# A four-block transformer kernel: attention features from three split parts stacked on 96 rows by on-chip copies, norm chain moved up in the step

## The chip, the core and the metric

The kernel runs on one core of a Trainium2 chip. The metric is the device time of one execution in microseconds (us), lower is better. The core has a matrix engine (TensorE, PE in the profile, whose weight loads are listed apart as PEld), a vector engine (VectorE, DVE), a scalar engine (ScalarE, ACT), a general engine (GpSimd, POOL) and a queue engine (SyncE, SP) that here only issues DMAs. Each engine works through its own list of instructions in order; they meet through semaphores, on which an instruction waits until a count is reached.

## What is computed

Four blocks, each followed by a residual add and a layer norm: a state-space mixer, a dense feed-forward, a linear attention with random features, and a feed-forward with 8 routed and 2 shared experts. The change is in the attention. Its reference, cut to what matters (batch 4, 1024 tokens, width 256, 16 heads of 16; M = 32 directions, R = 2 nodes, so 64 features for each head):

```python
def _features(x, omega, quad_nodes, quad_weights):
    xn = x / jnp.maximum(jnp.linalg.norm(x, axis=-1, keepdims=True), 1e-12)
    proj = jnp.einsum('bhtd,rhdm->rbhtm', xn, omega)
    s = quad_nodes[:, None, None, None, None]
    arg = jnp.clip(proj * jnp.sqrt(2.0 * jnp.maximum(s, 0.0)) - s, -20.0, 20.0)
    feat = jnp.exp(arg) / np.sqrt(M).astype(np.float32)
    feat = feat * jnp.sqrt(jnp.maximum(quad_weights, 0.0))[:, None, None, None, None]
    return jnp.transpose(feat, (1, 2, 3, 0, 4)).reshape(B, H, T, R * M)
qkv = x @ Wqkv + bqkv
q, k, v = jnp.split(qkv, 3, axis=-1)
qf = _features(q, omega, quad_nodes, quad_weights)
kf = _features(k, omega, quad_nodes, quad_weights)
# causal linear attention over chunks of 128 tokens:
#   ctx = qf . cumsum(kf v), den = max(qf . cumsum(kf), 1e-6), out = ctx / den
return out @ Wout + bout
```

## The kernel before

The program runs in phases with a barrier of all engines between them: `phase_mixer` (the first two blocks), `phase_attention`, `phase_shared` and `phase_experts`. A matrix product in fp32 accuracy is made of fp32r parts: an operand x is split into a high part (a copy by ACT) and a low part (x minus high, by DVE), and three products high.high, high.low and low.high are added up in PSUM (`PARTS`).

`phase_attention` goes through 8 steps of 128 tokens x 4 batch entries (`body(i)`, with a ninth body that empties the pipeline). A step has 8 turns t = 0 to 7, one for each pair of heads. In turn t the matrix engine computes

- `features` of pair t: queries and keys of two heads against the directions, 2 banks of 512 columns;
- `scores` and `turn_keys` of pair t-1, then `context` of pair t-2;
- and the step's other work, the "x steps", placed by the table `SLOTS_OF_X` at three points of a turn: A after the features, B after the scores, C after the context.

The x steps are: `FT` 0, 1 (turn the input rows), `FQ` 0 to 3 (project queries and keys, one for each batch entry), `FV` (values), `FN` 0 to 3 (turn the normed queries and keys into columns: 0 and 2 hold pairs 0 to 3 of queries and keys, 1 and 3 pairs 4 to 7), `BO` (turn the context back), `BC` and `BW` (output projection). `FT`, `FQ`, `FN` 0 and `FN` 2 are made one step ahead. Two PSUM banks, used in rotation, hold the results; DVE's `x_evac` frees them (`x_free`), for `FT`, `FN` and `BC` after ACT's `x_high`.

Between `FQ` and `FN` lies the norm chain. POOL squares queries and keys in two halves (L1308, after `FQ` 1 and `FQ` 3), DVE sums them (`squares`, L1670), makes a first guess of the inverse root (`norm_guess`, L1675 to L1677) and three Newton steps (`norm_newton`, L1680 to L1682), POOL multiplies (L1313, two instructions, one for `FN` 0 and 2 and one for `FN` 1 and 3). DVE's list in a turn is: `clip` of pair t (L1651, reads the features' banks), x step A, `mask` of pair t-1 (L1656), x step B, `new_state`, x step C, with the norm pieces between. ACT's list is: `x_high` of A, `exponentials` of pair t (L1520), `key_rows`, `x_high` of B, `context_out`, `x_high` of C.

There is one pair of feature banks, one pair of score banks and one context bank: `features` of the next pair waits for this pair's `clip`, `scores` for the last `mask`. The normed columns lie in one tile `qkt` of 128 rows (8 heads x 16) by parts, with keys rolled by 32 rows so that the two products of a pair use different rows. `features` (L1419) then issues six matmuls on 32 rows each:

```python
rows = [slice(2 * HD * at, 2 * HD * (at + 1)) for at in (t % 4, (t + 1) % 4)]
for c, (lp, rp) in enumerate(PARTS):
    for q in range(2):
        mm = pe.matmul(ps[:, FB + q, :], om[rows[q], lp, t, :], qkt[rows[q], rp, KD * q + t // 4, :],
                       start=c == 0, stop=c == 2)
```

Beside this POOL and ACT split the routed experts' weights, four blocks of 512 KB in each of steps 1 to 6 (POOL: L1287, then a store L1289 and a load L1291 by DMA). SP loads the next rows, stores finished rows, and at the phase's start loads the six blocks of shared weights (L1246), which the next phase uses.

## Time and profile before

| | us |
|---|---|
| median of 3 runs | 1459.89 (1459.82 to 1463.75) |
| the profiled execution | 1448.13, span 1446.5 |
| `phase_mixer` | 0 to 325.6 |
| `phase_attention` | 325.6 to 773.6 |
| `phase_shared` and `phase_experts` | 773.6 to 1446.5 |
| one step of attention (544.04 to 599.70) | 55.66 |
| PE busy in that step | 53.60 |
| DVE, ACT, POOL busy in that step | 43.36, 27.61, 26.60 |

The profile shows one execution, 11.8 us under the median of the runs without one. Its rows give for each engine when a group of like instructions started, how long it was busy, and in brackets how long the engine had been idle before and what released it. A matmul's end is modelled, so for groups on PE the distance from start to start says what a group costs. Busy time of an engine says little by itself; what counts is whether something waits for it.

### The profile page before, as it was taken

How to read it: one execution, taken by the hardware profiler on the slowest of the kernel's cores; microseconds unless marked ns; L12 is line 12 of the kernel's file. 1: busy time of each engine (PE TensorE's matmuls, PEld its weight loads, DVE VectorE, ACT ScalarE, POOL GpSimd, SP SyncE). 2: the span in 40 equal slices, each digit the busy share in tenths (PEclk: the TensorE clock that was granted, in tenths of full speed). 3: DMA queues.
4: the chain of work that ended last, by engine and by line, in shares of the span. 5: the costliest groups of instructions: out<-in, count | busy, mean ns of one | idle time of the engine just before them, and what ended most of it. 6: DMA issues, size and time to landing. Idle time of an engine off the chain costs nothing. (4 is left out here: it accounts for less than half of the span.)

```text
span 1446.5 us, 33923 instructions
## 1 busy us (share of the span) xinstructions
PE 1371.3 (95%) x12256; PEld 1190.8 (82%) x12256; DVE 914.3 (63%) x1944; ACT 684.4 (47%) x1257; POOL 551.6 (38%) x503
## 2 busy tenths in 40 slices
PE   6989999989999999999998999999999999999994
PEld 5778888877677777777777988888899999999984
DVE  4666767676776877877774464444555555555547
ACT  2356667544545455445444433223355555555533
POOL 0144555442254354454310006422344444444421
PEclk9799999998999999999999999999999999999997
DMA  6333333105133133233115204633788888888885
GB/s 223 128 136 123 111 133 128 52 15 181 45 100 120 57 117 123 65 131 102 45 60 219 104 30 162 263 111 122 188 227 233 234 233 234 233 234 234 248 258 213
DMA packets 103869, 216.12 MB, mean 149 GB/s; under 512 B 18544, under 2 KB 74224, under 8 KB 96624
## 3 DMA queue, kind: packets, MB, share of 16 engines
q1 hardware_dynamic: 79552, 159.87, 33.8%
q0 software_dynamic: 23088, 54.31, 13.1%
q8 instruction: 47, 0.77, 0.2%
q10 hardware_dynamic: 1152, 0.93, 0.2%
q14 instruction: 30, 0.25, 0.1%
HBM read 150.23 MB, written 64.84 MB: 149 GB/s over the span
## 5 line engine op out<-in xcount | busy, mean ns | idle before, releaser
L2637 PE MATMUL ps<-e_xhl,s_whl 128*128 128x256 f32 x1848 | 245.7, 282 | 0.0
L2637 PEld LDWEIGHTS ps<-e_xhl,s_whl 128*128 128x128 f32 x1848 | 231.0, 189 | 0.2 <-issue 0.2
L2019 PE MATMUL ps<-s_xhl,s_whl 128*128 128x512 f32 x660 | 164.5, 398 | 1.4 <-PEq L1108 1.4
L2468 POOL DMA_INDIRECT xs<-e_y,e_slot_id x78 | 122.1, 1566 | 90.5 <-ACT e_y L2502 71.4
L492 POOL TENSOR_TENSOR b_hhl<-b_h,b_hhl 128x512 fp32r<-128x512 f32 x64 | 94.7, 1482 | 139.7 <-ACT b_hhl L756 118.3
L2019 PEld LDWEIGHTS ps<-s_xhl,s_whl 128*128 128x128 f32 x660 | 122.1, 190 | 26.5 <-issue 1.8
L2616 PE MATMUL ps<-s_whl,e_ghl 128*128 128x256 f32 x936 | 139.3, 285 | 0.6 <-issue 0.6
L2716 DVE TENSOR_TENSOR e_g<-ps,e_act_h 128x256 f32<-128x256 f32 x156 | 66.2, 424 | 112.8 <-ACT e_act_h L2515 112.8
L2616 PEld LDWEIGHTS ps<-s_whl,e_ghl 128*128 128x128 f32 x936 | 121.8, 189 | 0.8 <-issue 0.7
L589 PE MATMUL ps<-b_w,b_hhl 128*128 128x256 f32 x768 | 105.3, 287 | 6.3 <-DVE b_turned_rows L862 5.6
L2515 ACT ACTIVATE e_act_h<-ps 128x256 f32<-128x256 f32 x156 | 60.1, 385 | 107.9 <-PE ps L2637 102.4
L589 PEld LDWEIGHTS ps<-b_w,b_hhl 128*128 128x128 f32 x768 | 99.2, 192 | 11.7 <-issue 6.0
L576 PE MATMUL ps<-b_xhl,b_w 128*128 128x512 f32 x384 | 104.4, 407 | 0.1
L1520 ACT ACTIVATE c_qf<-c_cf,fc 128x512 f32<-128x512 f32 x64 | 46.2, 722 | 117.9 <-DVE c_cf L1651 117.9
L1287 POOL TENSOR_TENSOR c_elo<-c_eraw,c_ehi 128x1024 fp32r<-128x1024 f32 x24 | 57.2, 2385 | 107.0 <-ACT c_ehi L1537 99.3
L2730 DVE TENSOR_TENSOR e_ghl<-e_g,e_ghl 128x256 fp32r<-128x256 f32 x156 | 67.8, 435 | 41.8 <-ACT e_ghl L2525 41.8
L2009 PE MATMUL ps<-s_whl,d_ghl 128*128 128x256 f32 x672 | 90.2, 283 | 1.8 <-DVE d_ghl L2251 1.6
L2009 PEld LDWEIGHTS ps<-s_whl,d_ghl 128*128 128x128 f32 x672 | 86.7, 188 | 6.2 <-ACT d_ghl L2105 1.8
L2245 DVE TENSOR_TENSOR d_g<-ps,d_act_h 128x512 f32<-128x512 f32 x56 | 38.7, 690 | 83.5 <-PE ps L2019 69.8
L1651 DVE TENSOR_SCALAR c_cf<-ps,fc 128x1024 f32<-128x1024 f32 x64 | 85.6, 1338 | 4.8 <-PE ps L1419 4.4
L2525 ACT ACTIVATE e_ghl<-e_g 128x256 fp32r<-128x256 f32 x156 | 64.7, 415 | 46.8 <-DVE e_g L2716 46.8
L2461 POOL CAST s_whl<-wall 128x1024 fp32r x38 | 39.5, 1041 | 119.3 <-PE ps L2616 109.4
(384 smaller groups left out, 2737.2 us busy)
## 6 DMA issues: line engine op xcount, KB each, us to landing
s_whl<-wlo SPq DMA_DIRECT2D x38, 1024.0 KB, 5.0
s_whl<-wlo SPq DMA_DIRECT2D x38, 512.0 KB, 3.7
c_eraw<-in_expert_w POOLq DMA_DIRECT2D x24, 512.0 KB, 4.9
wlo<-c_elo POOLq DMA_DIRECT2D x24, 512.0 KB, 3.0
wall<-in_expert_w SPq DMA_DIRECT2D x8, 1536.0 KB, 9.2
xg<-b_zeros POOLq DMA_DIRECT2D x13, 780.0 KB, 3.9
e_xr<-xg SPq DMA_DIRECT2D x39, 260.0 KB, 3.8
x<-rows_out SPq DMA_DIRECT2D x16, 512.0 KB, 3.2
```

Source lines behind the costliest of these rows:

```text
L492: gp.tensor_tensor(hhl[:, m % 4, 1], h[:, m % 4], hhl[:, m % 4, 0].bitcast(F32), ALU.subtract).then_inc(s["hlo_ready"], 1)
L576: mm = pe.matmul(ps[:, H + m % 2, :], w1s[:, wp, kd, m * P:(m + 1) * P], xhl[:, k, xp, kd, :], start=q == 0, stop=q == 3 * KD - 1)
L589: mm = pe.matmul(ps[:, O + b // 2, lo:lo + D], hhl[:, m % 4, hp, b * P:(b + 1) * P], w2s[:, wp, m, :], start=m == 0 and q == 0 and b % 2 = ...
L1651: ve.tensor_scalar(cf[:, u % 2], ps[:, FB:FB + 2, :], fc[:, HIGH], fc[:, LOW], ALU.min, ALU.max).then_inc(s["clip_done"], 1)
L2009: mm = pe.matmul(ps[:, O + b // 2, (b % 2) * D:(b % 2 + 1) * D], ghl[:, m % 4, gp_, b * P:(b + 1) * P], whl[:, wp_, m // HM, lo:lo + D], s ...
L2019: mm = pe.matmul(ps[:, H + 2 * (m % 2) + w, :], whl[:, wp, e, lo:lo + P], xhl[:, k, xp, kd, :], start=q == 0, stop=q == 3 * KD - 1)
L2468: gp.indirect_dma_start(xs, bass.IndirectOffsetOnAxis(ap=slot_id[:, i, b:b + 1], axis=0), y[:, k, b, :], None, compute_op=ALU.add).then_in ...
L2525: act.activation(ghl[:, m, 0], g[:, m], ACT.Copy).then_inc(s["ghi_ready"], 1)
L2616: mm = pe.matmul(ps[:, O + k, b * D:(b + 1) * D], ghl[:, m, gp_, b * P:(b + 1) * P], whl[:, k, wp_, lo:lo + D], start=m == 0 and q == 0 an ...
L2637: mm = pe.matmul(ps[:, H + m, w * SLOT:(w + 1) * SLOT], whl[:, k, wp, lo:lo + P], xhl[:, k, xp, kd, :], start=q == 0, stop=q == 3 * KD - 1)
L2716: ve.tensor_tensor(g[:, m], ps[:, H + m, SLOT:2 * SLOT], act_h[:, m], ALU.mult).then_inc(s["g_ready"], 1)
L2730: ve.tensor_tensor(ghl[:, m, 1], g[:, m], ghl[:, m, 0].bitcast(F32), ALU.subtract).then_inc(s["glo_ready"], 1)
```

## The change

- `features` multiplies once for each bank: a stationary operand of 96 rows (high, low, high of the directions, prepared by the host as one block repeated four times on 128 rows and split so that rows 32 to 63 hold the low part) against a moving operand `fs` of 96 rows that holds high, high, low of a pair's normed columns. Two matmuls for a pair in place of six.
- `fs` is filled by DMAs. `FN` results are split into a tile `stage`; `stack_pair` then copies, for each pair, three blocks of 32 rows x 2 x 512 values (128 KB each) from `stage` to `fs` on SP's queue: 12 copies for each half of a step (`stack(i+1, 0)` after `FN` 2, `stack(i, 1)` after `FN` 3). `features` waits for its pair's three copies, and ACT's `x_high` of `FN` 1 and of `FN` 0 waits until the four pairs copied last from `stage` have landed.
- The x steps are placed anew: `FQ` 0 to 3 in turns 2 and 3 (before in 3 and 4), `FN` 0 and 2 in turn 6 (before in 7), `BO` 0 and 1 one turn later. `squares` and `norm_guess` stand in turn 4, the Newton steps in turn 5. On POOL the squares come before the third weight block.
- The tiles `gm`, `bs`, `st`, `bt`, `ct` of the mixer, and `stage`, share memory with rows that are used later. The first four pairs of step 0 are copied at the mixer's end. Four of the six blocks of shared weights are loaded at the end of attention, since `fs` uses their place. SP's stores of finished rows come one body later.

Cut to its core:

```diff
+def stack_pair(sp, ahead, t):
+    g = t % QUAD
+    for n, part in enumerate((0, 0, 1)):
+        sp.dma_start(ahead.fs[t // QUAD][n * MF:(n + 1) * MF, g].bitcast(F32), ahead.stage[g * MF:(g + 1) * MF, part].bitcast(F32)).then_inc(ahead.stacked[t], 16)
...
+                if is_(i, STEPS + 1):
+                    sp.wait_ge(s["fn_lo"], 2)
+                    for t in range(QUAD):
+                        stack_pair(sp, ahead, t)
...
-                      2: ((A_, "FT", 0), (B_, "FT", 1), (C_, "BO", 3)),
-                      3: ((A_, "FQ", 0), (B_, "FQ", 1), (C_, "BC", 1)),
-                      4: ((A_, "FQ", 2), (B_, "FQ", 3), (C_, "BW", 0)),
-                      5: ((A_, "BW", 1), (C_, "BO", 0)),
-                      6: ((A_, "BO", 1),),
-                      7: ((A_, "FN", 0), (B_, "FN", 2))}
+                      2: ((A_, "FT", 0), (A_, "FT", 1), (B_, "BO", 3), (C_, "FQ", 0)),
+                      3: ((A_, "FQ", 1), (B_, "FQ", 2), (C_, "FQ", 3), (C_, "BC", 1)),
+                      4: ((B_, "BW", 0),),
+                      5: ((A_, "BW", 1),),
+                      6: ((A_, "BO", 0), (B_, "FN", 0), (C_, "FN", 2)),
+                      7: ((C_, "BO", 1),)}
...
+            def stack(i, half):
+                k1 = (i, "FN", 3) if half else (i - 1, "FN", 2)
+                sp.wait_ge(s["x_free"], x_index(*k1) + 1)
+                for t in range(QUAD * half, QUAD * (half + 1)):
+                    if not isinstance(i, int) or i > 0:
+                        sp.wait_ge(s["feat_done"], 2 * (PAIRS * (i - 1) + t + 1))
+                    stack_pair(sp, ahead, t)
...
+                if last_rows(i):
+                    sp.wait_ge(s["feat_done"], 2 * PAIRS_ALL)
+                    for n in range(2, NCH):
+                        load_shared(n)
...
+                pe.wait_ge(stacked[t], STACKED * (i + 1))
                 wait(pe, "clip_done", n)
...
+                for q in range(2):
+                    pe.matmul(ps[:, FB + q, :], om[0:STACK, t, :], fs[t // QUAD][0:STACK, t % QUAD, q, :],
+                              start=True, stop=True).then_inc(s["feat_done"], 1)
...
+                        if name == "FN" and a < KD:
+                            for before in range(QUAD * (1 - a), QUAD * (2 - a)):
+                                act.wait_ge(stacked[before], STACKED * (i + 1))
...
+                    if front and t == 4:
+                        squares(norm, i + 1, 0)
                     if front and t == 5:
-                        squares(norm, i + 1, 1)
-                        norm_guess(norm)
                         norm_newton(norm, False)
...
                     if front and t == 4:
-                        squares(norm, i + 1, 0)
+                        squares(norm, i + 1, 1)
+                        norm_guess(norm)
```

Where instructions stand now, at the three places that matter. On PE in the loop's body of attention, turn 6 of a step (features, then `c_ot` is `BO`, `c_qf` scores, `ident,c_kf` turned keys, `c_va` to `c_sm` the context). Before:

```order
L1419 MATMUL ps<-s_qkt,early 128x512 x6
L1235 REGISTER_ALU
L1395 MATMUL ps<-ident,c_ot 128x128 x4
L1425 REGISTER_ALU
L1431 MATMUL ps<-c_qf,c_kf 128x128 x8
L1437 MATMUL ps<-ident,c_kf 128x128 x4
L1451 MATMUL ps<-c_va,c_kr 64x32 x8
```

The same turn in the changed kernel (`s_fs` is the stacked operand, `s_sq` the normed rows that `FN` turns):

```order
L1459 MATMUL ps<-s_fs_53,early 128x512 x2
L1254 REGISTER_ALU
L1439 MATMUL ps<-ident,c_ot 128x128 x4
L1463 REGISTER_ALU
L1469 MATMUL ps<-c_qf,c_kf 128x128 x8
L1475 MATMUL ps<-ident,c_kf 128x128 x4
L1254 REGISTER_ALU
L1429 REGISTER_ALU
L1433 MATMUL ps<-ident,s_sq 128x128 x4
L1489 MATMUL ps<-c_va,c_kr 64x32 x8
```

`FN` 0 now stands in turn 6 between the turned keys and the context; before, it stood in turn 7 behind the features. On DVE, from the clip of turn 4 to the clip of turn 5, in the changed kernel (`s_nrm<-s_sq` is `squares`, `c_sm` the mask, `s_zz` the evacuation of `BW` 0):

```order
L1697 TENSOR_SCALAR c_cf<-ps,fc 128x1024
L1714 REGISTER_ALU
L1716 TENSOR_REDUCE s_nrm<-s_sq 128x64
L1702 TENSOR_TENSOR c_sm<-ps,s_tri 128x1024
L1647 REGISTER_ALU
L1675 TENSOR_TENSOR s_zz<-ps,c_xb 128x512
L1708 TENSOR_TENSOR c_state<-ps,c_state 128x128
L1714 REGISTER_ALU
L1716 TENSOR_REDUCE s_nrm<-s_sq 128x64
L75 ISA
L1721 TENSOR_SCALAR s_nrm<-s_nrm 128x128
```

Both sums now come in turn 4, one of them ahead of the mask; before, the second came behind the clip of turn 5. On SP the end of the mixer and the start of attention, before:

```order
L452 DMA x<-rows_out 128x4x256
L244 UNCONDITIONAL_BRANCH
L1237 UNCONDITIONAL_BRANCH
L1240 DMA s_tri<-in_masks 128x128
L1241 DMA c_bout<-in_bout 128x256
```

and in the changed kernel:

```order
L466 DMA x<-rows_out 128x4x256
L229 DMA s_fs_52<-s_stage 32x1024 x12
L258 UNCONDITIONAL_BRANCH
L1256 UNCONDITIONAL_BRANCH
L1259 DMA s_tri<-in_masks 128x128
L1260 DMA c_bout<-in_bout 128x256
```

Twelve copies stand ahead of the barrier that ends the mixer.

## Rows read from the trace of the kernel before

**Rows 1.** Windows: us of window, busy of each engine, PEclk (granted clock), DMA share, GB/s.
```profile
544.04:599.70 55.66, 53.60 (x713) 40.45 (x714) 43.36 (x82) 27.61 (x48) 26.60 (x31) 1.00 0.31 104
```
**Rows 2.** Timeline (start, us, engine line op): PE, turn 3, features, FQ 0, scores.
```profile
563.73 0.97 PE L1419 MATMUL ps<-s_qkt,early 32*128 32x512 f32 x6
564.82 1.66 PE L1358 MATMUL ps<-early,s_xts 128*128 128x512 f32 x6
566.41 1.16 PE L1431 MATMUL ps<-c_qf,c_kf 64*128 64x128 f32 x16
```
**Rows 3.** Timeline: PE, BC 0 of turn 1, features of turns 5 and 6.
```profile
550.86 0.66 PE L1398 MATMUL ps<-ident,c_cr 128*128 128x128 f32 x4
...
580.76 0.96 PE L1419 MATMUL ps<-s_qkt,early 32*128 32x512 f32 x6
...
587.28 0.96 PE L1419 MATMUL ps<-s_qkt,early 32*128 32x512 f32 x6
```
**Rows 4.** Timeline: PE, turn 7 and the start of the next step.
```profile
592.84 0.96 PE L1419 MATMUL ps<-s_qkt,early 32*128 32x512 f32 x6 [0.54 <-DVE c_cf L1651]
593.73 0.66 PE L1389 MATMUL ps<-ident,s_sq 128*128 128x128 f32 x4
594.89 1.16 PE L1431 MATMUL ps<-c_qf,c_kf 64*128 64x128 f32 x16 [0.50 <-DVE c_sm L1656]
...
599.70 0.49 PE L1419 MATMUL ps<-s_qkt,early 32*128 32x512 f32 x2 [0.88 <-DVE s_qkt L1599]
```
**Rows 5.** Timeline: DVE, turn 5: clip, second sum, Newton step, mask.
```profile
582.60 1.34 DVE L1651 TENSOR_SCALAR c_cf<-ps,fc 128x1024 f32<-128x1024 f32 x1
...
584.45 1.21 DVE L1670 TENSOR_REDUCE s_nrm<-s_sq 128x64 f32<-128x1024 f32 x1
...
586.48 0.29 DVE L1680 SCALAR_TENSOR_TENSOR s_nrm<-s_nrm 128x128 f32<-128x128 f32 x1
...
587.46 1.22 DVE L1656 TENSOR_TENSOR c_sm<-ps,s_tri 128x1024 f32<-128x1024 f32 x1
```
**Rows 6.** Timeline: POOL, normed rows, and the store of the fourth weight block.
```profile
590.78 3.83 POOL L1313 TENSOR_TENSOR s_sq<-s_qk,s_nrm 128x1024 f32<-128x1024 f32 x2 [9.07 <-DVE s_nrm L1682]
...
597.60 0.60 POOL L1289 DMA_DIRECT2D wlo<-c_elo  x1 [0.67 <-POOL c_elo L1287]
```
**Rows 7.** Timeline: ACT in turn 0, high parts of FN 1 and FN 3, exponentials.
```profile
545.64 0.60 ACT L1513 ACTIVATE s_qkt<-ps 128x512 fp32r<-128x512 f32 x1 [2.03 <-PE ps L1389]
546.78 0.72 ACT L1520 ACTIVATE c_qf<-c_cf,fc 128x512 f32<-128x512 f32 x1 [0.54 <-DVE c_cf L1651]
...
548.50 0.58 ACT L1513 ACTIVATE s_qkt<-ps 128x512 fp32r<-128x512 f32 x1
```
**Rows 8.** Timeline: DVE, low part of FN 2.
```profile
598.87 0.69 DVE L1599 TENSOR_TENSOR s_qkt<-ps,s_qkt 128x512 fp32r<-128x512 f32 x1 [0.64 <-ACT s_qkt L1513]
```
**Rows 9.** One line's DMAs of 128 KB on SP: ns min/median/max, and landing.
```profile
L388 SPq DMA_DIRECT2D b_grown<-drow x16: 472/508/633, 26.4 to 214.6; - x16
...
DMA to landing us min/median/max: 2.7/3.3/11.1
```
**Rows 10.** One line's stores of 8 and 24 KB on SP, and landing.
```profile
L393 SPq DMA_DIRECT2D arow<-b_turned_rows x2: 343/350/356, 21.2 to 71.3; - x2
...
DMA to landing us min/median/max: 1.4/1.4/1.4
```
**Rows 11.** Timeline: end of the mixer, last low parts on DVE, first features.
```profile
323.00 1.27 DVE L1030 TENSOR_TENSOR s_qkt<-ps,s_qkt 128x512 fp32r<-128x512 f32 x2
...
325.60 1.65 PE L1419 MATMUL ps<-s_qkt,early 32*128 32x512 f32 x6 [3.60 <-PEq L1103]
```
**Rows 12.** Timeline: PE, first router product of the phase behind attention.
```profile
777.75 1.92 PE L1988 MATMUL ps<-wall,d_xts 128*128 128x8 f32 x16 [0.89 <-DMA d_ones<-in_masks]
```
**Rows 13.** Windows around the mixer's end: the granted clock is the third value from the right.
```profile
316.00:320.00 4.00, 0.37 (x4) 0.17 (x2) 3.85 (x6) 0.00 (x0) 2.87 (x2) 0.91 0.00 0
320.00:326.00 6.00, 2.37 (x10) 2.00 (x12) 4.25 (x5) 1.20 (x2) 1.97 (x2) 0.50 0.00 0
```

99 lines of the change are left out of this document (51 added, 48 removed).

## The prediction

> **What bounds the kernel now.** I read the page first, then the windows, then the timeline of one steady step, engine by engine. In the step from 544.04 to 599.70 PE is busy 53.60 of 55.66 us at the full granted clock, DVE 43.36 [rows 1]. So attention runs at PE's pace, and a matmul taken away is worth its start-to-start distance as long as nothing else comes late. The reader should see second where PE does wait in the step: 0.54 us for the clip and 0.50 us for the mask in turn 7, 0.88 us for the low part of `FN` 2 at the next step's start [rows 4], and 0.2 us in turn 3, where the features take 1.09 us to the next start [rows 2] against the 0.89 of turn 7 [rows 4]. These 2.1 us are spots where DVE is a turn behind: from the clip at 582.60 on its rows leave no gap [rows 5] until the norm chain's end releases POOL at 590.78 [rows 6]. The change takes work off PE and none off DVE, and puts the norm chain closer to its user. The waits decide, not the count of matmuls.
>
> **The features.** Six matmuls on 32 rows cost 593.73 - 592.84 = 0.89, say 0.90 us [rows 4] (two run beside each other, since they use different rows). The two new ones use the same 96 rows, so they follow each other. The nearest row is `FQ`: six matmuls of 128x512 take 566.41 - 564.82 = 1.59 us, 0.265 each [rows 2], so two take 0.53. Saving 0.37 a pair, 64 pairs: -23.7 us. The Trainium skill, TensorE: Matmul & The Clock Gate, Part 1, gives 215.7 ns from start to start for such a matmul at the warm clock; by that figure two take 0.43 and the saving would be 30 us. The row in this kernel is slower and I stay with it. As bounds I take 0.30 to 0.45 a pair, 19 to 29 us.
>
> The unstalled step of before is 55.66 - 2.1 = 53.5 us; less 8 x 0.37 it is 50.6. If nothing else were late the seven steps after the first would give this: 23.7 + 6 x 2.1 = 36 us. Now what comes late.
>
> **The norm chain against `FN` 0.** `FN` 0 needs POOL's first product, which needs the last Newton step. Time on PE, from the start of turn 5: before, turn 5 takes 587.28 - 580.76 = 6.52 us [rows 3]; now 0.37 less, and without `BO` 0 (some 0.6), so 5.55. In turn 6 PE reaches `FN` 0 after features 0.53, `BO` 0 0.6, scores 1.1 and turned keys 0.6: 8.4 us after turn 5's start. On DVE the list from the clip of turn 4 to the chain's end is two clips with an evacuation each (582.60 to 584.45, 1.85 each), two sums and the first guess (584.45 to 586.48 is one sum with the guess, 2.03, and 1.2 for the other), two masks (1.15 each), three Newton steps (587.46 - 586.48, 0.98 each) and two state updates with a wait for ACT (0.9 in all) [rows 5]: 3.7 + 3.2 + 2.3 + 2.9 + 0.9 = 13.0. It can begin when `BC` 1's low part is done, 1.4 us into turn 4 (an ACT copy of 0.60 and a DVE subtraction of 0.69 and the hops [rows 7, 8]). Turn 4 is also some 5.55 us. So the chain ends 1.4 + 13.0 - 5.55 = 8.85 us into turn 5, POOL's first product takes half of 3.83 [rows 6], and `FN` 0 can start at 10.8 in place of 8.4: **a new wait of 2.4 us**. Before, the chain ended at 590.7 and `FN` 0 came only at 593.73 [rows 4, 6]. The squares on POOL are no limit: they now stand ahead of the third weight block. Six steady steps: +14.4. Bounds 1 to 3.5 a step.
>
> **The copies.** `FN` 2 is now PE's last work in turn 6; its low part is done 1.4 us into turn 7. Turn 7 before takes 599.70 - 592.84 = 6.86, of which 1.4 are waits [rows 4]; less 0.37, and with one `BO` in place of two `FN`, it is 4.6 us. So 3.2 us are left for the first copies, and none of this kind is in the trace. Nearest rows: 128 KB on SP take 0.51 us to issue (0.47 to 0.63) and 2.7 to 3.3 us to land out of HBM [rows 9]; small stores take 0.35 us and 1.4 us [rows 10]. I take 0.55 an issue, back to back, and 2.5 us to land (nearer to the row of the same size, a bit below it because both ends are on the core). Pair 0: 0.2 + 2 x 0.55 + 2.5 = 3.8, so the step starts 0.6 us late. All four pairs: 0.2 + 11 x 0.55 + 2.5 = 8.75, 10.15 us into turn 7. Until then ACT's list stands still at the high part of `FN` 1; behind it are queued the exponentials of pair 0, `key_rows` of pair 7 and the high part of `FN` 3. From there: ACT copy 0.65, exponentials and key rows 548.50 - 546.78 = 1.72, copy 0.58 [rows 7], low part 0.69 and hops 0.2: `FN` 3's bank is free 3.85 us later, 14.0 us into turn 7. PE wants that bank for `BC` 0, before 6.82 us into the step (550.86 - 544.04 [rows 1, 3]), now 6.1, that is 4.6 + 6.1 = 10.7 into turn 7. **PE loses 3.3 us** at each passage to a new step, 0.6 at the start and the rest at `BO` 2 and `BC` 0. Seven passages: +23. Bounds: 0 with small-store numbers, 6 with a landing later by 3 us. The 12 copies of the other half have two turns more and are hidden by turns 1 to 3; what would cost is only their place on SP's queue, ahead of the load of rows for `FT`, which is due a step later. The low part of `FN` 1 holds DVE up too (clip, then this, then the mask): the mask of pair 7 is then due in turn 1, where PE waits already.
>
> **The edges.** The last low part of the mixer ends at 324.3 and the first features start at 325.6 [rows 11]. Now SP first issues 12 copies, 12 x 0.55 = 6.6 us less the 0.4 in which the others arrive: the barrier is late by +6.2 (4 to 7.5). At the other end four loads of 512 KB follow attention's last store; the router's first product waited at 777.75 for a small load issued behind the barrier [rows 12], and that now queues behind 2 MB: +2.5 (1 to 5). Step 0 has no `BW` and `BC`, so PE reaches `FN` 0 even earlier, but it waited there before as well: +1 (0 to 3). Moving the mixer's tiles, the host's new layout and the fewer rows of the low part of the directions cost nothing on any path.
>
> **The sum**, against the profiled execution (1448.13): -23.7 - 6 x 2.1 (12.6) + 14.4 + 23 + 6.2 + 2.5 + 1 = +10.8. I take off 1.5 for turn 3's and turn 7's waits in step 0 and step 7, which partly go too: +9.3. The profiled execution lies 11.8 us under the median; I put the same difference on the median: 1459.89 + 9.3 = **1469.2 us**, 0.6% slower. Two measurements of this kernel can be told apart from about 0.3%, 4.4 us.
>
> **Rivals.** (1) *The copies are quick.* With 0.35 to issue and 1.7 to land, the step starts on time, all four pairs are there after 0.2 + 3.85 + 1.7 = 5.75 us, and PE loses 0.4 at a passage; the first edge shrinks to 12 x 0.35 - 0.4 = 3.8: -23.7 - 12.6 + 14.4 + 2.8 + 3.8 + 2.5 + 1 - 1.5 = -13.3, 1446.6, faster. For it: the copies never touch HBM. Against: 12 in a row, and the row of the same size. This is the other side, and it decides at the landing of the twelfth copy: each us earlier than mine is worth 7 us, until 5.5 us.
> (2) *The copies are slow.* POOL's fourth weight block stands behind both products. Before, its store came 597.60 - 590.78 = 6.8 us after they began [rows 6]; now they begin 8.85 us into turn 5, so its store and load, 1 MB, start some 2 us into turn 7, just when the copies do. If the twelfth lands 3 us later still, 7 x 3 = +21: 1490. The Trainium skill, SBUF — State Buffer, section on the DMA port swizzle, says that a transfer on 32 partitions reaches 8 of the 16 ports and gives 189 GB/s for 1 MiB; by that the twelve copies (1.57 MB) would need 8.3 us of transfer alone where my issues take 6.6, so it speaks for this rival and against the change. No row here shows a copy between 32 partitions.
> (3) *The norm chain is in time*, because DVE starts turn 4 earlier or POOL's product is quicker: then 6 x 2.4 fall away, 1455. Against: DVE's rows are without a gap and their durations do not vary.
> (4) *The clock falls.* It went from 1.00 to 0.50, half of full speed, after PE had been idle for most of 316 to 320 [rows 13]. My waits are 2.4 us and shorter, so mostly not; if they do it at some passages, 2 to 3 us each, 1480 to 1490.
>
> **How the numbers follow.** Forecast 0.41 (1462 to 1477), rival 1 0.23, rival 2 0.19, rival 3 0.11 (half of it over 0.3% faster), rival 4 0.06. Faster by over 0.3% (under 1455.5): 0.23 + 0.05 = 0.28. Within 0.3%: 0.06 from rival 3 and 0.09 from the low end of the forecast, 0.15. Slower: 0.57. The range reaches from inside rival 1 to rival 2's time: 1445 to 1490.
>
> **What the profile after would show.** Two matmuls of 96x512 with 0.53 us to the next start (wrong if 0.6 or more). In turn 6 a wait of PE before `FN` 0 released by POOL's product, 2.4 us. DVE without a gap from turn 4 to the end of turn 5. SP: twelve issues of 0.5 us after `FN` 2, landing 2 to 3 us each. ACT idle in turn 0 until the twelfth lands, then PE waiting before `BO` 2 and `BC` 0, 3 us in all. First features 6 us later than 325.6. A step of 50.6 + 2.4 + 3.3 = 56.3 us. If the step is 53 us, the copies or the chain were quicker than I have it; if it is 59, the copies share the engines with POOL's transfers.

## The result and the profile after

The changed kernel takes **1516.43 us** (median of 4 runs, 1514.39 to 1517.87); the kernel before took 1460.68 us (1459.82 to 1463.75, 4 runs) beside it. The ratio is 1.0377, 95% interval 1.0357 to 1.0397: 3.8% slower. The forecast was 1469.2 with a range to 1490, so the direction was right and the size was missed by 47 us.

The profiled execution of the changed kernel, and its steady step (from the first features of one step to the first of the next), stretch by stretch: length, busy time of PE, PEld, DVE, ACT and POOL, granted clock, DMA share, GB/s. The first line is the counterpart of [rows 1].

```profile
569.78:630.92 61.14, 54.52 (x680) 42.84 (x681) 43.55 (x80) 27.64 (x48) 26.48 (x30) 0.92 0.51 146
618.00:625.50 7.50, 7.40 (x74) 5.56 (x74) 4.19 (x6) 2.62 (x6) 6.80 (x6) 0.54 0.18 70
640.00:646.00 6.00, 6.00 (x86) 5.16 (x85) 3.88 (x6) 3.15 (x5) 1.68 (x1) 1.00 0.92 205
```

A step takes 61.14 us, 5.5 more than before, with 33 matmuls fewer in the record (680 for 713). PE is *busier* than before (54.52 against 53.60 us): matmuls were taken away, and where the granted clock falls to half of full speed those that are left last longer. The second stretch is such a place: mean granted clock 0.54. The third is one in which only the copies move data, at 205 GB/s.

What the clock takes shows in the six steps from the second on, in the changed kernel and then in a run that is told below, e_two_matmuls, which issues as many matmuls of the same shapes, in the old slots and without the copies:

```profile
381.94:750.20 368.26, 322.19 (x4081) 253.16 (x4081) 257.85 (x466) 163.78 (x284) 155.35 (x165) 0.92 0.50 141
```

```profile
373.96:696.73 322.77, 296.39 (x4084) 235.44 (x4080) 255.69 (x467) 163.49 (x285) 155.01 (x165) 1.00 0.31 101
```

For the same number of matmuls PE is busy 322.2 us at a mean granted clock of 0.92 and 296.4 us at 1.00: 26 us more. It stands idle 46.1 us in place of 26.4. (A matmul's end is modelled, so this is about right and not exact.)

What PE waits for, over the whole program (in total, times, longest):

```profile
PE ps L1459 <- DMA s_fs<-s_stage: 20.5, 7, 4.8
PE ps L1433 <- POOL s_sq L1357: 13.2, 6, 2.2
PE ps L1459 <- PEq L1122: 11.6, 1, 11.6
PE ps L1439 <- DVE s_xts L1645: 7.0, 5, 1.5
PE ps L1439 <- DVE s_stage L1645: 5.8, 2, 3.5
...
PE ps L2035 <- DMA d_ones<-in_masks: 4.3, 1, 4.3
```

Line by line: the features wait for the copies; `FN` 0 waits for POOL's product; the first features wait behind the barrier after the mixer; `BO` 3 waits for `FT` 0's bank and `BO` 2 for `FN` 3's; the router waits for a small load. The same in order of time, from turn 6 on, on PE (start, us, line, what is multiplied, and in brackets the wait before and its end):

```profile
615.25 0.66 PE L1475 MATMUL ps<-ident,c_kf 128*128 128x128 f32 x4
618.10 0.72 PE L1433 MATMUL ps<-ident,s_sq 128*128 128x128 f32 x4 [2.20 <-POOL s_sq L1357]
618.75 1.07 PE L1489 MATMUL ps<-c_va,c_kr 128*64 128x32 f32 x16
...
623.67 1.96 PE L1469 MATMUL ps<-c_qf,c_kf 64*128 64x128 f32 x16
625.57 0.66 PE L1475 MATMUL ps<-ident,c_kf 128*128 128x128 f32 x4
...
630.92 0.72 PE L1459 MATMUL ps<-s_fs,early 96*128 96x512 f32 x2 [2.38 <-DMA s_fs<-s_stage]
631.48 0.60 PE L1433 MATMUL ps<-ident,s_sq 128*128 128x128 f32 x4
632.01 1.94 PE L1469 MATMUL ps<-c_qf,c_kf 64*128 64x128 f32 x16
```

The reader should see two waits of 2.2 and 2.4 us, and after each the same instructions at about half speed for some microseconds: the sixteen score matmuls take 1.96 and 1.94 us, against 1.16 elsewhere in the step. Beside it POOL, SP and ACT:

```profile
622.92 0.59 POOL L1331 DMA_DIRECT2D wlo<-c_elo  x1 [0.67 <-POOL c_elo L1329]
623.53 0.53 POOL L1333 DMA_DIRECT2D c_eraw<-in_expert_w  x1
...
624.37 21.91 SPq L229 DMA_DIRECT2D s_fs<-s_stage  x24
...
635.13 0.60 ACT L1560 ACTIVATE s_stage<-ps 128x512 fp32r<-128x512 f32 x1 [6.72 <-DMA s_fs<-s_stage]
```

POOL's store and load (1 MB) are issued 1.45 and 0.84 us ahead of the first copy. That copy is issued at 624.37, the third has landed at 630.92 (6.5 us, where the forecast had 0.55 x 2 + 2.5 = 3.6), and the twelfth at 635.1 (10.8 us, forecast 8.55). ACT's list stands still for 6.72 us. All copies by line, issue time and time to landing (min, median, max), and who waited:

```profile
L229 SPq DMA_DIRECT2D s_fs<-s_stage x192: 507/591/1971, 323.5 to 768.4; - x192
...
  ACT s_stage L1560: 52.6, 7
...
DMA to landing us min/median/max: 2.2/2.4/9.4
```

The issue (0.59) and the undisturbed landing (2.4 us) are what I had assumed (0.55 and 2.5). The landing up to 9.4 is not.

One number must be settled first. The first profile of before lay 11.8 us under its median. **e_before_again** is that kernel once more.

> The kernel before once more, unedited, for a second profiled execution. The first one (1448.1 us) lay 11.8 us under the median of the others, and the profiles of the changed kernel, of the norm part alone and of the stacking alone all show some 11 us in the shared phase in which PE's instructions start about 0.7 us apart without waiting for a semaphore, which the first profile of before doesn't show. If this stretch belongs to the kernel before as well: span near 1459, the stretch in the shared phase, attention as before (55.65 us a step). If it is a cost of the change: span near 1447 again, without it.

It took 1472.58 us (one run, span 1470.9), while the kernel before beside it had a median of 1466.0. Its attention is the old one (steps of 55.64 us, last features at 751.31 against 751.63); all the difference lies behind. The same stretch in the shared phase, first execution, then this one:

```profile
880.00:900.00 20.00, 20.00 (x114) 17.42 (x113) 8.44 (x12) 5.53 (x9) 15.61 (x16) 1.00 0.52 178
```

```profile
880.00:900.00 20.00, 11.55 (x47) 7.84 (x46) 2.77 (x4) 1.86 (x3) 15.44 (x17) 0.81 0.28 99
...
PE ps L2009 <- issue: 10.5, 11, 2.2
```

PE waits for no semaphore there, its instructions just come slowly. So this stretch belongs to the kernel before as well, and my carrying the 11.8 us over to the median was right. It goes with the chip, it seems: the experiments were made in five groups, each on a chip of its own, and the kernel before had medians of 1461.7, 1466.0, 1461.9, 1446.3 and 1465.4 us in them. In the fourth group all 16 executions of before took 1441 to 1451 us, and the four traces from it (e_late_only, e_late_warm, e_late_edges, e_all_mends) lack the stretch; in the other four groups before took 1459 to 1472 us and every trace has it. What makes it is not known. Below I therefore compare **ratios to the kernel before beside the run**, and 0.1% is 1.5 us. The last column of the table is a second measure, which leaves out all that lies behind attention: the time from the first to the last features in the trace of the run. The two traces of the kernel before give 426.0 and 426.1 us there, on times that lie 24 us apart.

### The profile page after: what moved, and what is told of

Read it like the earlier page. It is cut to its first block and busy times, and to the rows that moved or that the text cites. A ratio compares the mean times of both kernels' runs of the same rounds, so it can differ in the third digit from the quotient of the medians.

```text
span 1516.3 us, 33677 instructions
## 1 busy us (share of the span) xinstructions
PE 1378.1 (91%) x12000; PEld 1205.1 (79%) x12000; DVE 914.5 (60%) x1944; ACT 683.9 (45%) x1257; POOL 547.4 (36%) x503
## 3 DMA queue, kind: packets, MB, share of 16 engines
q0 software_dynamic: 23088, 54.31, 12.6%
## 5 line engine op out<-in xcount | busy, mean ns | idle before, releaser
L2066 PE MATMUL ps<-s_xhl,s_whl 128*128 128x512 f32 x660 | 170.3, 406 | 5.3 <-PEq L1127 2.6
L2056 PEld LDWEIGHTS ps<-s_whl,d_ghl 128*128 128x128 f32 x672 | 87.9, 191 | 12.6 <-issue 7.3
L1469 PEld LDWEIGHTS ps<-c_qf,c_kf 64*128 64x128 f32 x1024 | 69.8, 207 | 24.3 <-issue 18.6
L1469 PE MATMUL ps<-c_qf,c_kf 64*128 64x128 f32 x1024 | 82.6, 306 | 6.3 <-DVE c_sm L1702 4.1
```

Of the source, the lines that this page charges most:

```text
L1469: mm = pe.matmul(ps[:, SC + h, cols], kf[f, u % 4, cols], qf[f, u % 4, cols], start=True, stop=True)
L2056: mm = pe.matmul(ps[:, O + b // 2, (b % 2) * D:(b % 2 + 1) * D], ghl[:, m % 4, gp_, b * P:(b + 1) * P], whl[:, wp_, m // HM, lo:lo + D], s ...
L2066: mm = pe.matmul(ps[:, H + 2 * (m % 2) + w, :], whl[:, wp, e, lo:lo + P], xhl[:, k, xp, kd, :], start=q == 0, stop=q == 3 * KD - 1)
```

## The experiments

| run | ratio to before | 95% interval | first to last features, us |
|---|---|---|---|
| the kernel before | 1 | | 426.0 |
| the changed kernel | 1.0377 | 1.0357 to 1.0397 | 462.4 |
| e_norm_only | 1.0130 | 1.0101 to 1.0159 | 440.2 |
| e_two_matmuls | 0.9902 | 0.9876 to 0.9928 | 409.8 |
| e_stack_only | 1.0404 | 1.0377 to 1.0430 | 467.3 |
| e_pool_early | 1.0390 | 1.0351 to 1.0429 | 462.3 |
| e_warm | 1.0376 | 1.0354 to 1.0397 | 465.4 |
| e_spread | 1.0406 | 1.0362 to 1.0450 | 464.1 |
| e_two_queues | 1.0185 | 1.0166 to 1.0204 | 443.0 |
| e_bo_first | 1.0386 | 1.0363 to 1.0409 | 467.7 |
| e_shared_early | 1.0309 | 1.0287 to 1.0332 | 462.2 |
| e_late_only | 1.0286 | 1.0262 to 1.0309 | 448.7 |
| e_late_fn | 1.0146 | 1.0123 to 1.0169 | 429.0 |
| e_best | 1.0155 | 1.0124 to 1.0185 | 439.6 |
| e_late_warm | 1.0086 | 1.0064 to 1.0109 | 420.5 |
| e_late_edges | 1.0103 | 1.0081 to 1.0126 | 439.2 |
| e_all_mends | 1.0045 | 1.0030 to 1.0060 | 428.2 |
| e_ft_apart | 1.0025 | 1.0004 to 1.0045 | 423.1 |
| e_final | 1.0031 | 1.0013 to 1.0050 | 424.4 |

**The three parts of the change apart.** First the two matmuls, without copies:

```diff
-                for c, (lp, rp) in enumerate(PARTS):
-                    for q in range(2):
-                        mm = pe.matmul(ps[:, FB + q, :], om[rows[q], lp, t, :], qkt[rows[q], rp, KD * q + t // 4, :],
+                for q in range(2):
+                    pe.matmul(ps[:, FB + q, :], om[0:96, 0, t, :], qkt[0:96, 0, KD * q + t // 4, :],
```

> The kernel before with its six feature matmuls on 32 rows replaced by two on 96 rows that read the keys and queries where they already lie: no copies, no stacking, old slots and norm chain. It leaves out the low parts of the product and takes rows of the wrong heads, so its output is not the features' product; it times PE's side of the change by itself. Forecast's term: 0.37 us a pair (0.33 by the rows of the changed kernel), 64 pairs, -21 to -24; if DVE's lateness of 2.1 us a step stays or grows (DVE is a turn behind in turns 3, 4 and 7), less. Step 52.7 to 53.5 with the waits staying, 1437 to 1443 us; if all that is saved on PE turns into waits for DVE, 1455 to 1461.

0.9902, so **-14 us**. Its steady step, and two waits of turn 6:

```profile
588.86:642.92 54.06, 49.44 (x680) 39.23 (x681) 43.05 (x82) 27.50 (x48) 26.55 (x31) 1.00 0.33 107
...
632.05 1.16 PE L1427 MATMUL ps<-c_qf,c_kf 64*128 64x128 f32 x16 [1.21 <-DVE c_sm L1652]
...
636.07 0.74 PE L1417 MATMUL ps<-s_qkt,early 96*128 96x512 f32 x2 [0.54 <-DVE c_cf L1647]
```

PE's busy time falls from 53.60 to 49.44, 4.16 us or 0.52 a pair, more than my 0.37. But the step falls by 1.6 only: PE idles 54.06 - 49.44 = 4.62 us in place of 2.06, for DVE. Over attention its waits for the mask (`c_sm`) rise to this, where the kernel before had 4.5 us, 8 times:

```profile
PE ps L1427 <- DVE c_sm L1652: 14.4, 14, 1.4
```

Second, the norm chain and the slots alone, with the squares and the guess on DVE and the weight blocks on POOL where the change has them:

```diff
-                      6: ((A_, "BO", 1),),
-                      7: ((A_, "FN", 0), (B_, "FN", 2))}
+                      6: ((A_, "BO", 0), (B_, "FN", 0), (C_, "FN", 2)),
+                      7: ((C_, "BO", 1),)}
...
-                    split_expert_weights(i, range(1, EPER - 1))
+                    split_expert_weights(i, range(1, 2))
...
+                    split_expert_weights(i, range(2, EPER - 1))
```

> The kernel before with one part of the change alone: the new slots of the projections (FN 0 and FN 2 in turn 6, both FT in point A of turn 2), the norm chain moved up on DVE and the norm products' place on POOL. Features stay six matmuls on 32 rows, no copies. Forecast's terms: FN 0 then waits for POOL's first product, about 2.0 us a step (PE comes to it 0.7 us later than in the changed kernel, since its features are longer), the 0.9 us wait for the low part of FN 2 at a step's start goes: 6 x 1.1 = +7, 1467 us, step 56.8. Rival (what the trace of the changed kernel suggests): the wait also brings the clock down to half for some 6 us of PE work (+2 a step), and BO 3 waits 1.4 us for FT 0's bank: 6 x 4.5 = +27, 1487 us, step 60. If the norm part were harmless and all of the loss lay in the copies: 1455 to 1460.

1.0130, **+19 us**, between the forecast's +7 and the rival's +27. The step is 57.8 us in place of 55.65:

```profile
609.48:667.29 57.81, 54.87 (x714) 41.29 (x714) 43.54 (x81) 27.71 (x48) 26.54 (x30) 0.97 0.30 99
...
657.99 0.66 PE L1391 MATMUL ps<-ident,s_sq 128*128 128x128 f32 x4 [1.98 <-POOL s_sq L1315]
...
660.00 1.08 PE L1464 MATMUL ps<-c_sm,c_va 128*32 128x128 f32 x16
```

The sum by rows of that step: +1.98 for `FN` 0, +0.96 for `BO` 3's bank (a wait at 627.88), +1.27 busy time at a lower clock, less before's 2.06 of waits, all of which are gone here: +2.15, and the step is 57.81 - 55.66 = 2.15 longer. The wait for POOL is what I forecast; the clock and the bank I had left out.

Third, the stacking in the old slots: the changed kernel with the old `SLOTS_OF_X`, norm chain and POOL order, the diff above read backwards.

> The changed kernel with the old slots, the old place of the norm chain on DVE and of the products on POOL: only the stacking is left. FN 2 is then at point B of turn 7, so the first copies can be issued only some 4 us later than in the changed kernel. No FN 0 wait, no BO 3 wait. If the landing of the copies is what costs (6.5 us to the third, in place of my 3.6): a wait of about 6 us at each step's start with the clock falling after it, less the 2.2 + 1.4 + 1.5 that the norm part costs in the changed kernel: step about 62 to 63, 1525 us. If the norm part costs most of the 56 us that the changed kernel lost: 1490 us or less. By my recorded forecast (landing 2.5 us, no clock fall) the wait would be 3.5 us at the start, the rest as before: step 57 to 58, 1480 us.

1.0404, **+59 us**, worse than the whole change: the third copy comes 7 us after PE wants it.

```profile
635.32 1.21 PE L1457 MATMUL ps<-s_fs,early 96*128 96x512 f32 x2 [6.96 <-DMA s_fs<-s_stage]
```

Features -14 and norm chain +19 make +5; the whole change is +55, so some 50 us come with the copies (and the two edges, which every kernel with copies has). The parts don't add up: features and stacking in the old slots are +59, with the norm part's 19 that would be 78, and the whole is 55. Moving `FN` 2 ahead costs 19 us by itself and nothing here, where it lets the copies start sooner.

**POOL's megabyte, the clock, the order of the copies.** Moving POOL's fourth block ahead of the norm products:

```diff
-                    split_expert_weights(i, range(2, EPER - 1))
+                    split_expert_weights(i, range(2, EPER))
...
-                if not isinstance(i, int) or 1 <= i < LAST:
-                    split_expert_weights(i, range(EPER - 1, EPER))
```

> The changed kernel with one edit: POOL's fourth weight block (store and load, 1 MB) comes ahead of the norm products, in the 8 us in which POOL waits for DVE's chain, not behind them, where it starts 0.2 us before the first copies. Theory A (POOL's megabyte in front delays the copies, my rival 2): the third copy lands some 4 us after its issue in place of 6.5, the wait at the step's start falls from 2.4 us to nearly 0 with its clock fall, ACT's high part of FN 1 comes 2 us sooner: 3 to 4 us a step, 6 x 3.5 = -21, about 1495 us. Theory B (the copies are slow by themselves, half rate for 32 rows and 0.59 us an issue): within 4 us of the changed kernel, 1512 to 1520. If POOL's split of the block is too long for the gap, FN 0 waits longer and the time goes up: 1525.

No gain: 1.0390. But the trace shows that the theory was right on the third copy and blind to what is late next:

```profile
623.23 14.23 SPq L229 DMA_DIRECT2D s_fs<-s_stage  x14
...
626.92 0.73 PE L1457 MATMUL ps<-s_fs,early 96*128 96x512 f32 x2 [0.70 <-DMA s_fs<-s_stage]
634.12 0.65 PE L1437 MATMUL ps<-ident,c_ot 128*128 128x128 f32 x4 [2.19 <-DVE s_stage L1643]
636.23 1.11 PE L1440 MATMUL ps<-ident,c_cr 128*128 128x128 f32 x4 [0.93 <-DVE s_stage L1643]
...
632.66 0.60 ACT L1558 ACTIVATE s_stage<-ps 128x512 fp32r<-128x512 f32 x1 [6.18 <-DMA s_fs<-s_stage]
```

With POOL's transfer out of the way the third copy lands 3.7 us after the first issue (my 3.6), and PE waits 0.70 in place of 2.38. The twelfth still lands after 9.4 us, ACT still stands for 6.18, and PE pays 2.19 + 0.93 at `BO` 2 and `BC` 0. The forecast had this second wait as the main one; POOL's block only hid it in the changed kernel. After it the clock falls, as the row of `BC` 0 shows: the four transposes of `c_cr` take 1.11 us, against 0.66 in [rows 3].

The clock: 8 matmuls of 96x512 added ahead of `FN` 0's wait and 8 ahead of the step's first wait for a copy.

```diff
+                    if name == "FN" and a == 0:
+                        for _ in range(8):
+                            pe.matmul(ps[:, xp, :], om[0:STACK, 0, :], xts[0:STACK, 0, 0, :], start=True, stop=True)
```

> The changed kernel with 8 added matmuls of 96x512 (2.1 us at full clock, results overwritten) ahead of FN 0's wait for POOL and ahead of each later step's first wait for the copies, so that PE works in about the time in which it stood. The waits themselves end when they ended before. Theory C (the clock's fall to half after these two waits costs about 3 us a step, 1.2 to 1.9 us for work that takes 0.6 to 1.1 otherwise): granted clock 0.98 or more in attention in place of 0.92 to 0.94, 6 x 2.5 = -15, 1500 us. If the clock had no part in the loss: 1516 or, where the added work outlasts the wait, up to 1522.

No gain either: 1.0376. The clock stays at 1.00 after `FN` 0, and the time is taken back at the next wait, which is 3.43 us although 2.1 us of added work stand ahead of it (in the changed kernel 2.38 with nothing ahead; the clock falls after it in both):

```profile
622.11:625.11 3.00, 3.00 (x54) 2.24 (x54) 1.54 (x3) 1.31 (x3) 2.97 (x2) 1.00 0.00 0
...
633.63 1.22 PE L1465 MATMUL ps<-s_fs,early 96*128 96x512 f32 x2 [3.43 <-DMA s_fs<-s_stage]
```

The first copy is issued 4.5 us after `FN` 0's start (620.91 to 625.37) in place of 6.3, and the third lands 8.3 us after that in place of 6.5: POOL's megabyte, issued at 625.75, comes when it came before, and the copies end when it lets them.

Two mends each without effect, while PE waits on and on at another place: the changed kernel has waits in series, and one of them alone gives its time to the next.

The order of the copies:

```diff
-                for t in range(QUAD * half, QUAD * (half + 1)):
+                for g in (0, 2, 1, 3):
+                    t = QUAD * half + g
...
-    for n, part in enumerate((0, 0, 1)):
+    for n in (0, 2, 1):
+        part = n // 2
```

> The run with POOL's block ahead of the products, and the copies only issued in another order: pairs 0, 2, 1, 3 and, in a pair, the rows 0 to 31, 64 to 95, 32 to 63. If a copy between 32 partitions is slow because it reaches half of the ports, and neighbours in the queue now lie on different halves, the twelfth lands 1 to 2 us sooner than 10.3 us after FN 2's low part begins, ACT's stall (6.2 us) gets shorter by that, step 1 to 1.5 us less: 1505 to 1510. If the queue works a copy off at its own rate (one issue each 0.59 us), whatever its rows: no change, 1513 to 1520.

1.0406 against 1.0390: no change. The rate of the copies with nothing beside them is 205 GB/s, at 0.92 of the DMA engines' time. The Trainium skill, SBUF — State Buffer, section on the DMA port swizzle, says that 32 partitions reach 8 of 16 ports and gives 189 GB/s at 1 MiB; the size of the rate agrees. That ports are the cause was not shown: the order that should have spread them moved nothing.

Four of the twelve copies on ACT's queue:

```diff
+                    if t == 6 and is_step(i + 1):
+                        act.wait_ge(s["x_hi"], next(h for _, _, m, b, _, h in x_events(i) if (m, b) == ("FN", 2)) + 1)
+                        act.wait_ge(s["feat_done"], 2 * (PAIRS * i + QUAD))
+                        for g in range(QUAD):
+                            stack_pair(act, ahead, g, (1,))
```

> The run with POOL's block ahead of the products, and one more edit: of the twelve copies at a step's end ACT issues the four of the second high part on its own queue right after FN 2's high part (it stands idle there for 2 us), SP the other eight. If the issue rate of one queue (0.59 us a copy) holds the twelfth copy up: it lands some 3 us sooner, ACT's high part of FN 1 starts 3 us sooner, the waits at BO 2 and BC 0 (2.2 + 0.9 us) go: step 57.5 to 58, 6 x 3 = -18, about 1498 us. If the transfers themselves are the limit (32 rows at 205 GB/s, twelve copies 7.7 us): the twelfth lands at most 0.5 us sooner, step 60 to 61, 1512 to 1518 us.

1.0185, by the ratios 30 us less than e_pool_early. The two runs are of different groups, and their traces have 19 us of it in attention (443.0 for 462.3), near the 18 of the first theory; where the rest lies I can't say. In its copies' stretch the rate is 248 GB/s, and ACT's stall falls from 6.18 to 3.84 us:

```profile
617.00:622.00 5.00, 4.41 (x72) 3.15 (x68) 3.18 (x8) 2.09 (x4) 0.00 (x0) 1.00 1.01 248
...
565.18 0.60 ACT L1559 ACTIVATE s_stage<-ps 128x512 fp32r<-128x512 f32 x1 [3.84 <-DMA s_fs<-s_stage]
568.75 0.66 PE L1441 MATMUL ps<-ident,c_cr 128*128 128x128 f32 x4 [0.99 <-DVE s_stage L1649]
```

The wait at `BO` 2 is gone and 0.99 at `BC` 0 is left. From the end of `FN` 2's high part to ACT's start at `FN` 1 it is 8.7 us in place of 10.3: 1.6 sooner, neither 3 nor 0.5. The one queue's rate holds part of it.

**Taking the twelfth copy off the path.** Instead of making it faster, `FN` 1 and `FN` 3 go to turn 1, since their rows are needed in turn 4 only:

```diff
-        SLOTS_OF_X = {0: ((A_, "FN", 1), (B_, "FN", 3), (C_, "BO", 2)),
-                      1: ((A_, "BC", 0), (C_, "FV", 0), (C_, "FV", 1)),
+        SLOTS_OF_X = {0: ((A_, "BO", 2), (C_, "BC", 0)),
+                      1: ((A_, "FN", 1), (B_, "FN", 3), (C_, "FV", 0), (C_, "FV", 1)),
```

> The run with POOL's block ahead of the products, with FN 1 and FN 3 moved from turn 0 to turn 1 (BO 2 and BC 0 one slot up), so that ACT's high part of FN 1 comes when all twelve copies have landed. My recorded mechanism: ACT's list stands still for the twelfth copy and PE loses at BO 2 and BC 0. Then these waits (2.2 + 0.4 to 0.9 us a step) and ACT's stall of 6.2 us go, only pair 0's three copies are left on the path: step 57.5 to 58.5, 7 x 3 = -21, about 1495 us. If the loss only moves on (features of pairs 1 to 3, or the norm chain, which starts from the same point of the step): within 5 us of 1517.

1.0146 against 1.0390: **36 us** back from this one edit, where I expected 21. A step (the six from the second on take 56.9 us on the mean, 61.4 before the edit):

```profile
551.03:607.48 56.45, 51.28 (x681) 40.21 (x681) 43.99 (x81) 27.40 (x48) 26.51 (x30) 0.97 0.58 158
...
557.36 0.60 ACT L1558 ACTIVATE s_stage<-ps 128x512 fp32r<-128x512 f32 x1 [0.40 <-PE ps L1431]
```

ACT now waits 0.40 us for PE and nothing for a copy. Why 36 and not 21: the six steps, without the edit (e_pool_early) and with it,

```profile
381.57:750.07 368.50, 322.50 (x4081) 252.09 (x4081) 261.03 (x465) 164.08 (x284) 155.57 (x165) 0.93 0.50 141
```

```profile
380.22:721.52 341.30, 310.40 (x4080) 244.00 (x4081) 261.53 (x465) 163.08 (x284) 155.41 (x165) 0.96 0.56 153
```

get 27.2 us shorter, of which 15.1 are idle time of PE and 12.1 are busy time at a higher granted clock; the last step gives 6.3 more, half and half. The waits alone, some 18 us, are about what I expected; most of the rest is the clock, which fell less often. The same edit on the changed kernel, with POOL's block where the change has it:

> The changed kernel with FN 1 and FN 3 in turn 1 alone (POOL's block behind the products, as the change has it). If ACT's stall for the twelfth copy is the cost by itself: the waits at BO 2 and BC 0 don't exist here in the changed kernel's trace beyond small ones, but the third copy still lands 6.5 us after its issue (2.4 us wait at the start, clock down after it): step 59.5, about 1500 us. If POOL's megabyte no longer matters: as e_late_fn, 1482. If the two act only together: 1510 or more.

1.0286. The steady step is still 61.77 us (61.26 in the changed kernel), since the third copy is late as before and the clock falls after it; the 13 us come from step 1 (57.05 us in place of 63.37) and the last one (38.2 us to its last features in place of 45.0).

```profile
623.17 1.22 PE L1459 MATMUL ps<-s_fs,early 96*128 96x512 f32 x2 [3.98 <-DMA s_fs<-s_stage]
```

So the two act together: POOL's block alone 0, `FN` 1 and 3 alone 13, both 34 us (1.0377 to 1.0146). This is the cause of most of the loss, 34 of 55 us: the megabyte makes the *third* copy late, the queue makes the *twelfth* late, and each stands behind the other.

**The waits that are left.** Now the clock again, where the copies no longer take it back (8 matmuls ahead of `FN` 0 only, otherwise e_late_fn):

> e_late_fn with 8 added matmuls of 96x512 ahead of FN 0's wait for POOL, so that PE's clock doesn't fall to half after it (2.2 us wait, then 2 to 5 us at half clock in the trace). In the changed kernel this gave nothing, because the wait for the copies took it back. If the clock costs 1 to 1.5 us a step and only the third copy is left behind it: PE comes to FN 2 0.5 us sooner, so half of it stays: step 56.5 against 57.2, 1476 to 1479 us. If all is taken back again by the copies: 1482.

1.0086, **9 us** less than e_late_fn (and 8.5 less in attention); the clock of the step shown is 1.00.

```profile
604.96:660.29 55.33, 51.59 (x689) 40.72 (x689) 44.07 (x81) 27.41 (x48) 26.54 (x30) 1.00 0.58 161
```

`BO` 3 ahead of `FT` 0 and 1 in the changed kernel:

```diff
-                      2: ((A_, "FT", 0), (A_, "FT", 1), (B_, "BO", 3), (C_, "FQ", 0)),
+                      2: ((A_, "BO", 3), (A_, "FT", 0), (B_, "FT", 1), (C_, "FQ", 0)),
```

> The changed kernel with the order BO 3, FT 0, FT 1 in turn 2 in place of FT 0, FT 1, BO 3, so that BO 3 has no bank to wait for. The wait of 1.43 us a step that I had not seen goes. If it costs what it shows: 7 x 1.4 = -10, 1506 us. If the step is a loop (step start, FQ, squares, Newton, FN 0, FN 2, copies, next start) and this wait is beside the loop: the 1.4 us come back before FQ 0 or FN 0, 1514 to 1519 us.

1.0386, no gain, and attention is 5 us longer in the trace: PE now waits 7.5 us over attention at `FT`, for the copy of `c_cr` on DVE that frees that bank, where it had waited 7.0 us at `BO` 3.

The edge at attention's end, the four shared loads ahead of the last store of `x3`:

```diff
+                if last_rows(i):
+                    sp.wait_ge(s["feat_done"], 2 * PAIRS_ALL)
+                    for n in range(2, NCH):
+                        load_shared(n)
                 if is_step(i - 2):
                     sp.wait_ge(s["out_ready"], PRIMED + i - 1)
```

> The changed kernel with one edit at attention's end: the four shared-weight loads of 512 KB are issued ahead of the last store of x3 and its wait, right after the last features, so that they are not in front of the small loads of the shared phase. Term of the forecast: this edge costs 2.5 us (5.1 by the trace of the changed kernel, where the router's first product waits 4.3 us for the ones). Expected: that wait back to about 1 us, 3 to 5 us less, 1512 us. Rival: the loads are not what holds it up, 1516.

1.0309, **10 us** less than the changed kernel. The wait of 4.31 us for `d_ones` is down to 0.34. Attention is the same (462.2 us for 462.4). In the changed kernel the granted clock is 0.66 from 820 to 840 us, in e_shared_early 0.83; so a part of the gain is likely to be that, but I did not take it apart.

**e_best** has all that was known by then, on two queues, with `BO` 3 first and the shared loads ahead:

> All mends together: POOL's block ahead of the products, four of the copies on ACT's queue, FN 1 and FN 3 in turn 1, BO 3 ahead of FT 0, the shared loads ahead of the last store. Left are the norm chain's wait at FN 0 (2.2 us a step), pair 0's copies (0.6 to 1.3), DVE's lateness, the first edge (+7). If the terms add up: 1493 for the two queues, -7 for BC 0's wait, -10 for the shared loads, up to -10 for BO 3: 1466 to 1476, still no faster than the kernel before. If the passage is a loop, the -7 and -10 inside the step give at most half: 1476 to 1484.

1.0155, no better than e_late_fn by itself, although the shared loads give their 10 us behind attention: in attention it is 10.6 us *longer* (439.6 for 429.0). Two mends of one cause don't add, and here they cost: PE waits 1.2 to 1.4 us for the third copy in five of its steps, against 0.35 to 0.72 in e_late_fn's later ones, and 9.0 us in all at `FT` behind `BO` 3, against 8.1 at `BO` 3. Which of the two edits costs how much was not taken apart.

The first edge: nine of the mixer's twelve copies issued after the barrier, first thing in attention (and the shared loads as above).

```diff
-                    for t in range(QUAD):
-                        stack_pair(sp, ahead, t)
+                    stack_pair(sp, ahead, 0)
...
+            for t in range(1, QUAD):
+                stack_pair(sp, ahead, t)
             sp.dma_start(tri[:], masks[0]).then_inc(s["weights_in"], 16)
```

> e_late_fn with both edges mended: the mixer issues pair 0's three copies only, the other nine are issued as the first thing of attention's SP; the four shared loads are issued ahead of the last store. Forecast's term for the first edge is 12 issues less 0.4 us, so nine issues less are 9 x 0.55 = -5; the second edge gave 9 to 10 us in e_shared_early. Sum: -14 to -15, about 1467 us, 0.4% over the kernel before. If the nine copies at attention's start hold up its first loads: -10 only, 1472.

1.0103, 6 us less than e_late_fn and no more than the shared loads had given. The first features come at 327.3 in place of 330.8, but step 0 takes 56.5 us in place of 49.5, because pair 1's copies now land late beside POOL's first megabyte:

```profile
336.43 1.22 PE L1458 MATMUL ps<-s_fs,early 96*128 96x512 f32 x2 [7.91 <-DMA s_fs<-s_stage]
```

So the first edge can't be mended in this way: the last features come at 766.5 us, later than the 759.7 of e_late_fn. All the gain of this run lies behind attention. With the 8 matmuls as well:

> e_late_edges with the 8 added matmuls ahead of FN 0's wait as well. By the sum of the terms 1467 - 4 = 1463 us: within 0.3% of the kernel before, no faster. Left then are the FN 0 wait (2.2 us a step), DVE's waits, and pair 0's copies. If it is under 1457, a mended version of the change beats the kernel before.

1.0045, **8 us** less than e_late_edges, as the same 8 matmuls gave before. Then turn 2 as before the change, `FQ` 0 at the head of turn 3:

```diff
-                      2: ((A_, "FT", 0), (A_, "FT", 1), (B_, "BO", 3), (C_, "FQ", 0)),
-                      3: ((A_, "FQ", 1), (B_, "FQ", 2), (C_, "FQ", 3), (C_, "BC", 1)),
+                      2: ((A_, "FT", 0), (B_, "FT", 1), (C_, "BO", 3)),
+                      3: ((A_, "FQ", 0), (A_, "FQ", 1), (B_, "FQ", 2), (C_, "FQ", 3), (C_, "BC", 1)),
```

> e_all_mends with turn 2 as the kernel before has it (FT 0, FT 1, BO 3 in points A, B, C) and FQ 0 at the head of turn 3. BO 3's wait (1.6 us) goes, and with it the half clock that follows it in some steps. If PE is the bound there: step 54 against 55.9, 7 x 1.6 = -11, ratio to the kernel before 0.997. If FQ 0 only comes later by what the wait took (the chain to FN 0 starts at the same time, the 8 added matmuls no longer cover the wait): ratio 1.003 to 1.006.

1.0025; the intervals of the two overlap (attention is 5.1 us shorter in the trace). Its steady step takes 54.94 us, 0.7 *less* than the kernel before:

```profile
549.13:604.07 54.94, 51.58 (x689) 40.64 (x689) 44.08 (x81) 27.27 (x48) 26.59 (x30) 1.00 0.58 162
```

Last, in **e_final**, POOL's first two loads (the two lines with `gp.dma_start(eraw[:, k], ...)`) moved behind `body(0)`:

> e_ft_apart, and POOL's first two loads of expert weights (1 MB) issued after step 0 in place of attention's start, where the nine copies of pairs 1 to 3 stand beside them. If the megabyte is what delays pair 1's copies by 7.9 us: step 0 takes 49 to 51 in place of 55.1 us, -4 to -6, ratio 0.3 to 0.4% lower than e_ft_apart, some 0.994 with the wait gone or 1.001 with it kept. If the copies are late for another reason: the same ratio as e_ft_apart.

1.0031, no gain. PE waits 2.36 us for pair 1's copies in place of 8.21, as the theory has it, but step 0 still takes 55.5 us (2.1 of it a new wait for a bank of `FN`), and a wait comes back at the next step's start, where the loads now are (3.93 us in place of 0.61):

```profile
332.57 1.22 PE L1461 MATMUL ps<-s_fs,early 96*128 96x512 f32 x2 [2.36 <-DMA s_fs<-s_stage]
...
384.46 0.91 PE L1461 MATMUL ps<-s_fs,early 96*128 96x512 f32 x2 [3.93 <-DMA s_fs<-s_stage]
```

No version of mine beats the kernel before. The best stands 0.25% over it, about the bound of what can be told: its attention is 2.9 us shorter, starts 2.7 us later for the first edge, and so ends where the old one did (751.4 and 751.6 us).

## Why the prediction was wrong, step by step

In short: the step that failed is the term of the copies, +23. It let a copy land 2.5 us after its issue whatever POOL's queue had in flight, and it let PE go on at full clock behind every wait. Measured were a third copy at 6.5 us, a twelfth at 10.8, and 26 us of busy time in six steps for a clock of 0.92. Term by term:

*The features, -23.7.* Mis-sized, and in the other direction than the result. PE's busy time fell by 0.52 a pair, 33 us, not 0.37. The distance from the features' start to the next start fell from 0.89 to between 0.47 and 0.57, near the forecast 0.53; but the groups beside them come closer too. In e_two_matmuls the features of turn 6 start 0.41 us after the transposes of `BO` 0 ahead of them (629.29 to 629.70), in the kernel before 0.58 us (586.70 to 587.28). Turn 5 got shorter by 6.52 - 5.81 = 0.71. The Trainium skill, TensorE: Matmul & The Clock Gate, Part 1, with 215.7 ns a matmul gave 30 us, nearer in the total; the rows have 0.47 to 0.57 us from a group of two to the next start, not 0.43. What it was worth is another matter: alone, 14 us.

*Before's waits, -12.6.* In e_two_matmuls they don't go, they double, since DVE is behind and PE only comes sooner. My own sentence, that the change takes work off PE and none off DVE, said so; the sum then took the waits off. In the changed kernel most of them are gone, replaced by larger ones.

*`FN` 0, +14.4.* Right in size: 6 waits, 13.2 us. Left out was what follows: half clock for some microseconds, which adds 1.3 us (the step of e_norm_only) to 3.0 (from `FN` 0 at 618.10 to 625.57 it is 7.47 us in the changed kernel; the same instructions take 4.46, 669.04 to 673.50, where the clock stays up in e_two_queues).

*The clock as an unlikely rival (0.06).* This was the second large error. I read [rows 13] as "idle for most of 4 us", and called waits of 2.4 us too short. Here the clock fell behind waits of 1.98 to 2.4 us in most steps, though not in all (in e_two_queues, after 2.20 us at 669.04, the next matmuls keep their 0.66). Price of the falls behind `FN` 0, where nothing hides it: 9 us (e_late_warm). All falls together, those behind the copies too: 26 us more busy time in six steps of the changed kernel.

*The copies, +23.* The mechanism (ACT's list stands for the twelfth copy, PE pays at `BO` 2 and `BC` 0) was right, and e_pool_early shows it as written, 2.19 + 0.93 + 0.70 = 3.8 us against 3.3. What failed is the landing time of 2.5 us for copies behind POOL's megabyte. My own row said that it could: [rows 9] has 2.7/3.3/11.1 us from issue to landing, and I took the first two and left out the 11.1. I had this as rival 2 at +21 and a chance of 0.19, weighed by the twelfth copy alone; it is the third that moves most (6.5 us against 3.6). Together with the order of `FN` 1 the whole block is worth 34 us.

*Turn 2.* Not in the prediction at all: both `FT` at point A, so `BO` 3 waits for a bank, 7.0 us in total. The order of the instructions showed it: between two users of one bank stood only one other. Its removal alone gave nothing (e_bo_first), and with turn 3 rearranged some 3 us by the ratios, 5 by the traces.

*The edges, +8.7.* First features +7.2 against +6.2, right. The second gave 10 us when mended, against my 2.5: I had put 2 MB ahead of a load of 64 KB and priced it as one wait.

*The sum.* Expected step 56.3, found 61.14; the six steps from the second on take 368.3 us where the forecast had 6 x 56.3 = 337.8, 30 more: 12 of idle time (46.1, where its terms were 6 x (2.4 + 3.3) = 34.2) and 18.6 of busy time (322.2, where 6 x 50.6 = 303.6 were left, and that although the features saved more than forecast). The last step, from its first to its last features, takes 45.0 us against 40.9 before the change: 4. The first edge 1 more than forecast, the second 7.5. That is 43 of the 47 us; the rest stays open.

*The point from which it decides.* Rival 1 needed a twelfth landing 3 us sooner than mine; e_late_fn makes that landing irrelevant, and the result is still +21 us. By the traces only 3 of these lie in attention (429.0 for 426.0) and 5 at the first edge, so the rest lies behind attention. And the 3 stand where the two matmuls alone would give -16 (409.8): `FN` 0's wait with its clock, DVE's lateness, `BO` 3's bank and pair 0's copies eat that. So quick copies would not have made this change faster, as far as e_late_fn tells; no run has copies that are quick.

## What to carry to other kernels

Price a matmul that is taken away by a run in which it alone is taken away, or else by who waits next: here 33 us of PE time gave 14, since DVE was a turn behind. When a copy is put between a producer and a tight consumer, look at what other queues have in flight at that moment, and at which engine's ordered list must stand until the *last* copy has landed; moving that instruction later gave 36 us, but 13 where the other queue's transfer still stood ahead of the copies. When a wait is priced, price the granted clock behind it too: count PE's busy time for the same matmuls before and after. When a mend changes nothing, look in the trace whether its own wait went: then a second one stands behind it, and both have to be mended in one run.

## What the runs showed of the hardware that I had not expected

A wait of PE of about 2 us is often followed by half the granted clock for the next microseconds. Behind the six waits of 2.20 us at `FN` 0 in the changed kernel it fell each time, behind the same waits in e_pool_early only in two of five; the sixteen matmuls of `c_va` and `c_state` then took 1.08 us in place of 0.64. With 2.1 us of added matmuls in that gap the clock stayed at 1.00 in the steps shown. So a wait of 2.2 us cost PE up to 2.2 + 3.0 = 5.2 us.

Copies between 32 partitions ran at 205 GB/s on one queue and 248 on two, with the DMA engines busy 0.92 and all of the time; a megabyte of another queue, issued about 1 us ahead of them, moved the third landing from 3.7 to 6.5 us behind the first issue.
